# Rotary tables multiplied by the reciprocal roots on GpSimd, in a projection stage of one stage less

## What is computed

```python
def apply_rotary(x, cos, sin):
    x1, x2 = (x[..., :d], x[..., d:])
    return jnp.concatenate([x1 * c + x2 * s, -x1 * s + x2 * c], axis=-1)
...
q = (x @ Wq.T).reshape(B, T, 2 * H, hd)
k = (x @ Wk.T).reshape(B, T, 2 * H, hd)
v = (x @ Wv.T).reshape(B, T, H, 2 * hd)
q = apply_rotary(rmsnorm(q), cos, sin)
k = apply_rotary(rmsnorm(k), cos, sin)
```

## Time and profile before

| | |
|---|---|
| median of three runs | 691.15 us (689.38 to 691.51) |
| span of the profiled execution | 687.9 us (the page gives no other time of it) |
| busy in the span: TensorE, VectorE, ScalarE, GpSimd | 590.2, 530.8, 496.5, 326.7 us |
| granted TensorE clock, mean | 0.950 |
| projection stage, last instruction | near 115.5 us |

### The profile page before, as it was taken

One profiled execution on the slowest core, in us unless ns is written; L12 is line 12 of the kernel. 1 busy time (PEld: TensorE's weight loads), 2 busy tenths in 40 slices (PEclk: granted clock), 3 DMA queues, 4 the chain that ended last, 5 costly groups with the idle time before them and its releaser, 6 DMA issues. The chain is left out here.

```text
span 687.9 us, 15892 instructions
## 1 busy us (share of the span) xinstructions
PE 590.2 (86%) x4825; PEld 355.3 (52%) x4826; DVE 530.8 (77%) x1425; ACT 496.5 (72%) x843; POOL 326.7 (47%) x466
## 2 busy tenths in 40 slices
PE   3576765899999999999999999977999799999960
PEld 2465554233333333333333333375877589999960
DVE  3999998687978889797888877779798856555575
ACT  2367795798989989898998999923455467777741
POOL 0224345344534344452434544252477777776661
PEclk9799998799999999999999999998899979999995
DMA  8000001000544566644466650041122233333475
GB/s 218 16 16 31 20 13 61 1 1 2 102 91 74 82 116 116 115 88 91 63 106 116 116 106 12 1 157 59 59 82 74 80 82 102 95 103 91 131 208 166
DMA packets 76265, 56.06 MB, mean 81 GB/s; under 512 B 6528, under 2 KB 70848, under 8 KB 75968
## 3 DMA queue, kind: packets, MB, share of 16 engines
q1 hardware_dynamic: 70688, 46.01, 30.8%
q0 software_dynamic: 4352, 8.99, 3.9%
q10 hardware_dynamic: 1184, 0.56, 0.3%
HBM read 15.36 MB, written 28.65 MB: 64 GB/s over the span
## 5 line engine op out<-in xcount | busy, mean ns | idle before, releaser
L787 ACT ACTIVATE attend_prob<-attend_ring 128x1024 f32<-128x1024 f32 (+1 forms) x320 | 280.0, 951 | 16.4 <-PE attend_ring L933 14.4
L731 POOL TENSOR_SCALAR_AFFINE_SELECT attend_prob<-attend_prob 128x256 f32<-128x256 f32 x256 | 118.0, 485 | 141.4 <-ACT attend_prob L787 140.8
L953 PE MATMUL attend_ps_o<-attend_prob,attend_v_slot 128*32 128x512 f32 (+3 forms) x1536 | 156.6, 496 | 0.0
L933 PE MATMUL attend_ring<-attend_qk_slot 32*128 32x512 f16 (+3 forms) x672 | 80.1, 329 | 8.1 <-ACT attend_prob L787 6.3
L1907 POOL DMA_INDIRECT expert_outputs<-routed_linear_gated,routed_expert_goal_now x72 | 70.3, 977 | 29.7 <-issue 23.9
L1033 POOL DMA_INDIRECT slots<-rows,slot_index x64 | 62.1, 971 | 37.3 <-issue 33.2
L933 PEld LDWEIGHTS attend_ring<-attend_qk_slot 32*128 32x128 f16 x672 | 22.4, 91 | 106.7 <-ACT attend_prob L787 37.6
L1935 DVE TENSOR_TENSOR outed_linear_head_normed<-outed_linear_head_normed,routed_linear_ps_c 128x256 f32<-128x256 f32 x72 | 30.2, 420 | 41.3 <-ACT outed_linear_head_normed L2029 36.8
L953 PEld LDWEIGHTS attend_ps_o<-attend_prob,attend_v_slot 128*32 128x32 f32 x1536 | 33.7, 108 | 44.9 <-issue 37.7
L2076 PE MATMUL routed_linear_ps_c<-outed_linear_head_normed,head_turned 128*128 128x128 f32 x384 | 52.5, 281 | 1.1 <-ACT head_turned L2010 1.1
L369 POOL TENSOR_TENSOR project_parts_q<-project_rotated_q,project_parts_q 128x1024 f16<-128x1024 f32 x8 | 17.6, 2201 | 68.9 <-ACT project_parts_q L417 68.9
(11 more groups left out here) (291 smaller groups left out, 1281.8 us busy)
## 6 DMA issues: line engine op xcount, KB each, us to landing
slots<-attend_zeros SPq DMA_DIRECT2D x24, 715.0 KB, 10.2
attend_qk_slot<-qk_parts SPq DMA_DIRECT2D x14, 512.0 KB, 3.1
x_pairs<-slots SPq DMA_DIRECT2D x72, 65.0 KB
v_all<-expert_outputs SPq DMA_DIRECT2D x8, 512.0 KB, 5.5
xn_all<-project_xn SPq DMA_DIRECT2D x8, 256.0 KB, 2.3
w<-w_laid SPq DMA_DIRECT2D x1, 2048.0 KB, 7.8
rows<-rows SPq DMA_DIRECT2D x4, 512.0 KB, 3.8
out<-xn_all SPq DMA_DIRECT2D x8, 256.0 KB, 3.5
```

Of the source, the lines that this page charges most:

```text
L731: ins = nc.gpsimd.affine_select(out=edge, in_=edge, compare_op=ALU.is_ge, fill=0.0, base=0, pattern=[[0, 2], [1, P]], channel_multiplier=-1)
L787: nc.scalar.activation(probs(k, pair)[:, :, 0:width], scores[:, :, 0:width], ACT.Exp, scale=HD ** -0.5).then_inc(exp_made[u][pair], 1)
L933: ins = nc.tensor.matmul(dst[:, s * QC + at:s * QC + at + cols], qk[rows, T + j * P:T + (j + 1) * P], qk[rows, qc * QC + off:(qc + 1) * QC ...
L953: ins = nc.tensor.matmul(ps_o[RB * s:RB * (s + 1), off:QC], v4[slot][:, j, s], probs(k, s // 2)[:, s % 2, at:at + cols], start=j == 0, sto ...
```

## The change

`body` loses its fourth group: turns have a (u+2), b (u+1) and c (u), and run from -2 to 7. In a turn, a is normalised, b is projected and rotated, and c is split in two parts, transposed and copied.

- The reciprocal roots no longer multiply q and k. GpSimd multiplies the tables of cosines and sines by them (four products of 128x256, two for each half), behind c's low parts in its queue, and VectorE multiplies q and k from PSUM by the results (`turn_half`, four passes of 128x512). PSUM of half h is free for the next projection when `half_turned[h]` is counted.
- The sum of squares, the root and the reciprocal are cut in halves of two tiles.
- VectorE's order in a turn: b's sums of squares, b's first reciprocal, a's statistics, b's second reciprocal, a's normalised x, b's four passes and b's four sums.
- ScalarE's: b's first square and v, c's high part of q, b's second square and first root, c's high part of k, b's second root and v, a's root, then the copies as before, of c now.
- TensorE's: behind b's projection six idle products, then the wait for c's low parts and c's quads 0 and 1, a's transposes, three idle products (there were three ahead of a's transposes and six behind them), c's quads 2 and 3.
- ScalarE takes a root of one number ahead of turn -2. The 4-bit rounding, steps 3 to 6, comes behind turn 6.

The core of the diff; the statistics and the normalised x of a are moved into functions (`statistics`, `normalise`) with nothing else changed, and `keep_v` is the copy of v.

```diff
-        sdev, rstd, pad = sb("sdev", GT), sb("rstd", GT), sb("pad", 1)
+        sdev, rstd, pad, warm = sb("sdev", GT), sb("rstd", GT), sb("pad", 1), sb("root_loaded", 1)
...
-        qkn = sb("qk_normed", GT * HQK * HD)
+        cos_n, sin_n = sb("cos_normed", GT * HQK * HD // 2), sb("sin_normed", GT * HQK * HD // 2)
...
-        squared = sem("squared")
-        qkv_made, v_kept, half_normed = ([sem(f"{n}{h}") for h in range(2)] for n in ("qkv_made", "v_kept", "half_normed"))
-        summed, rooted, rrms_made = (sem(n) for n in ("summed", "rooted", "rrms_made"))
-        turned = sem("turned")
+        squared = [sem(f"squared{h}") for h in range(2)]
+        qkv_made, v_kept, half_turned = ([sem(f"{n}{h}") for h in range(2)] for n in ("qkv_made", "v_kept", "half_turned"))
+        cos_made, sin_made = ([sem(f"{n}{h}") for h in range(2)] for n in ("cos_made", "sin_made"))
+        summed, rooted, rrms_made = ([sem(f"{n}{h}") for h in range(2)] for n in ("summed", "rooted", "rrms_made"))
...
-            return bcast(r[:, :, at:at + HD // 2], 2, 2 * HQK)
-
-        def halves(x):
-            return x.rearrange("p (t n d) -> p t n d", t=GT, d=HD // 2)
+            return bcast(r[:, :, at:at + HD // 2], 2, HQK)
+
+        half = lambda h: slice(h * GT // 2, (h + 1) * GT // 2)
+        by_head = lambda x: x.rearrange("p (t n) -> p t n", t=GT)
+        per_head = lambda x: x.rearrange("p (t n d) -> p t n d", t=GT, d=HD // 2)
+
+        def of_half(x, h):
+            n = x.shape[1] // 2
+            return x[:, h * n:(h + 1) * n]
...
-                body(*[(u + d, (odd + d) % 2) if inner or 0 <= u + d < GROUPS else None for d in (2, 1, 0, -1)])
+                body(*[(u + d, (odd + d) % 2) if inner or 0 <= u + d < GROUPS else None for d in (2, 1, 0)])
...
-            for u in range(GROUPS - 3, GROUPS + 1):
+            for u in range(GROUPS - 3, GROUPS):
...
-            def body(a, b, c, d):
...
-                    dve.wait_ge(half_normed[1], g + 1)
-                    nc.vector.tensor_tensor(halves(qcos), halves(qkn), rope(odd, 0), ALU.mult)
-                    nc.vector.tensor_tensor(halves(qsin), halves(qkn), rope(odd, HD // 2), ALU.mult).then_inc(turned, 1)
...
-                    dve.wait_ge(squared, 2 * g + 2)
-                    nc.vector.tensor_reduce(ssum, sq.rearrange("p (n d) -> p n d", d=HD), AX.X, ALU.add).then_inc(summed, 1)
+            def body(a, b, c):
                 if b:
                     g, odd = b
-                    dve.wait_ge(rooted, g + 1)
-                    nc.vector.reciprocal(rrms, sroot).then_inc(rrms_made, 1)
-                    dve.wait_ge(rrms_made, g + 1)
...
-                        dve.wait_ge(v_kept[h], g + 1)
-                        tiles = slice(h * GT // 2, (h + 1) * GT // 2)
-                        ins = nc.vector.tensor_tensor(qkn.rearrange("p (t h d) -> p t h d", t=GT, d=HD)[:, tiles], qk_psum[:, tiles],
-                                                      bcast(rrms.rearrange("p (t h) -> p t h", t=GT)[:, tiles], 3, HD), ALU.mult)
-                        ins.then_inc(half_normed[h], 1)
+                        dve.wait_ge(squared[h], g + 1)
+                        nc.vector.tensor_reduce(of_half(ssum, h), of_half(sq, h).rearrange("p (n d) -> p n d", d=HD), AX.X,
+                                                ALU.add).then_inc(summed[h], 1)
+                    unit_lengths(b, 0)
+                if a:
+                    statistics(a)
+                if b:
+                    unit_lengths(b, 1)
+                if a:
+                    normalise(a)
+                if b:
+                    g, odd = b
+                    for h in range(2):
+                        turn_half(b, h)
+                    add_halves(b)
+
+            def unit_lengths(group, h):
+
+                dve.wait_ge(rooted[h], group[0] + 1)
+                nc.vector.reciprocal(of_half(rrms, h), of_half(sroot, h)).then_inc(rrms_made[h], 1)
+
...
+            def normalise(group):
+
+                g, odd = group
+                dve.wait_ge(sdev_made, g + 1)
+                nc.vector.reciprocal(rstd, sdev).then_inc(rstd_made, 1)
+                dve.wait_ge(rstd_made, g + 1)
+                once(dve, xn_saved[odd], (g - odd) * 8)
+                once(dve, x_turned, g - 1)
+                for j in range(GT):
+                    ins = nc.vector.tensor_scalar(xn[odd][:, j * P:(j + 1) * P], m.x[:, ds(g * GN + j * P, P)],
+                                                  moments[:, 2 * j:2 * j + 1], rstd[:, j:j + 1], ALU.subtract, ALU.mult)
+                ins.then_inc(normed, 1)
+
+            def turn_half(group, h):
+
+                g, odd = group
+                by_pair = lambda x: of_half(x, h).rearrange("p (t n s d) -> p t n s d", t=GT // 2, s=2, d=HD // 2)
+                numbers = qk_psum[:, half(h)].rearrange("p t n (s d) -> p t n s d", s=2)
+                dve.wait_ge(v_kept[h], g + 1)
+                dve.wait_ge(cos_made[h], g + 1)
+                nc.vector.tensor_tensor(by_pair(qcos), numbers, bcast(per_head(cos_n)[:, half(h)], 3, 2), ALU.mult)
+                dve.wait_ge(sin_made[h], g + 1)
+                nc.vector.tensor_tensor(by_pair(qsin), numbers, bcast(per_head(sin_n)[:, half(h)], 3, 2),
+                                        ALU.mult).then_inc(half_turned[h], 1)
+
+            def add_halves(group):
+
+                g, odd = group
+                for h in range(2):
+                    dve.wait_ge(half_turned[h], g + 1)
+                once(dve, k_low, g)
+                cs = qcos.rearrange("p (t w h s d) -> p t w h s d", t=GT, w=2, s=2, d=HD // 2)
+                sn = qsin.rearrange("p (t w h s d) -> p t w h s d", t=GT, w=2, s=2, d=HD // 2)
+                for w in range(2):
+                    r = rot[w].rearrange("p (t h s d) -> p t h s d", t=GT, s=2, d=HD // 2)
+                    nc.vector.tensor_tensor(r[:, :, :, 0], cs[:, :, w, :, 0], sn[:, :, w, :, 1], ALU.add)
+                    nc.vector.tensor_tensor(r[:, :, :, 1], cs[:, :, w, :, 1], sn[:, :, w, :, 0],
+                                            ALU.subtract).then_inc(rotated[w], 1)
...
-                if u == GROUPS - 1:
+                if u == GROUPS - 2:
...
-                if u == GROUPS:
+                if u == GROUPS - 1:
...
-            def body(a, b, c, d):
+            def body(a, b, c):
...
+                if b:
+                    g, odd = b
+                    if isinstance(g, int) and g == 0:
+                        pool.wait_ge(rope_in, 16)
+                    for h in range(2):
+                        pool.wait_ge(rrms_made[h], g + 1)
+                        once(pool, half_turned[h], g)
+                        lengths = bcast(by_head(rrms)[:, half(h)], 3, HD // 2)
+                        nc.gpsimd.tensor_tensor(per_head(cos_n)[:, half(h)], rope(odd, 0)[:, half(h)], lengths,
+                                                ALU.mult).then_inc(cos_made[h], 1)
+                        nc.gpsimd.tensor_tensor(per_head(sin_n)[:, half(h)], rope(odd, HD // 2)[:, half(h)], lengths,
+                                                ALU.mult).then_inc(sin_made[h], 1)
...
+            def square(group, h):
+
+                g, odd = group
+                act.wait_ge(qkv_made[h], g + 1)
+                nc.scalar.activation(sq.rearrange("p (t c) -> p t c", t=GT)[:, half(h)], qkv4[:, half(h), 0:2 * C],
+                                     ACT.Square).then_inc(squared[h], 1)
+
...
+            def root(group, h):
+
+                act.wait_ge(summed[h], group[0] + 1)
+                nc.scalar.activation(of_half(sroot, h), of_half(ssum, h), ACT.Sqrt, bias=m.eps_rms[:, 0:1],
+                                     scale=1.0 / HD).then_inc(rooted[h], 1)
+
+            def body(a, b, c):
+                if b:
+                    square(b, 0)
+                    keep_v(b, 0)
+                if c:
+                    g, odd = c
+                    act.wait_ge(rotated[0], g + 1)
+                    nc.scalar.activation(part[odd][0][:, :, 0:2], bcast(rot_h[0], 2, 2), ACT.Copy).then_inc(q_high, 1)
+                if b:
+                    square(b, 1)
+                    root(b, 0)
+                if c:
+                    g, odd = c
+                    act.wait_ge(rotated[1], g + 1)
+                    nc.scalar.activation(part[odd][1][:, :, 0::2], bcast(rot_h[1], 2, 2), ACT.Copy).then_inc(k_high, 1)
+                if b:
+                    root(b, 1)
+                    keep_v(b, 1)
                 if a:
                     g, odd = a
                     act.wait_ge(mom_made, g + 1)
                     nc.scalar.activation(sdev, moments.rearrange("p (t k) -> p t k", k=2)[:, :, 1], ACT.Sqrt,
                                          bias=m.eps_ln[:, 0:1]).then_inc(sdev_made, 1)
...
+                if c and not b:
+                    keep(c, 0)
...
-                    keep(d, 2)
+                    keep(c, 2)
...
-                if d:
```

(53 more changed lines are left out.)

75 lines of the change are left out of this document (8 added, 67 removed).

## The result

The kernel after takes 711.09 us (median of 4 runs, 708.82 to 712.04), the one before 691.33 us (4 runs, 689.38 to 691.56) on the same chip: a ratio of 1.0295, 95% interval 1.0276 to 1.0313. It is slower, as forecast, but by 20 us instead of 10, outside the range. The span goes from 687.9 to 706.7 us. The next stage begins at 134.09 us (GpSimd's first memset there) against 116.63 before, 17.5 us later, and what follows takes 572.6 us against 571.3. So the loss lies in the projection stage. I call the start of that memset the stage's end from here on.

The account below looks back on a forecast made before the run. VectorE bounded the old turn of 10.85 us; the new chain, 11.0, plus 1.35 for low clock gave 12.35. 27.2 + 6 x 12.35 + 10.75 + 8.3 = 120.35 against 110.91; 691.15 + 9.8 = 701 us, range 696 to 705.

Parts of the forecast that it names:

- The chain in ScalarE's order: Per turn from first square (S) through high part, both low parts, transposes and copies to the next: 10.99 us.
- The idle stretch of 3.5 us: TensorE stands still from the end of its idle products, S + 2.6, to k's low part, S + 6.1.
- the copies' wait of 2.4: ScalarE idles about 2.4 us each turn in front of the copy of the first quad.
- the products of 0.6: GpSimd's four new 128x256 table products, behind the low parts, 0.6 us each, bounds 0.52 to 1.04.
- the passes of 0.65: VectorE's four new 128x512 passes from PSUM, 0.65 us each, 2.6 us together.
- The clock: TensorE's clock falls in nearly every turn, 0.7 us behind the restart, for 3.4 us; the turn grows by 1.35 us.
- low at every restart: Rival: TensorE's clock is already low when it restarts, turns of 13.1 us, 706 us in total; chance 0.12.
- 12.35: Forecast length of a turn in us: 11.0 at full TensorE clock plus 1.35 for the low clock.
- L271 beside GpSimd: Normalising of x beside GpSimd's low-part instruction: VectorE might lose 0.7 us, within its slack, so nothing changes.
- Start: Early Sqrt table takes a 1.28 us load out, all counting; first square of turn 0, S(0), at 27.2 us.
- Six turns: Turns 0 to 5 at 12.35 us each, bringing the first square of turn 6, S(6), to 101.3 us.
- Tail: After S(6): last sums at 10.75 us, fp4 steps 8.3 (bounds 5.3 to 8.93), rest as now, 0.2 more for low parts.

Follow-up runs that it names:

- g1: Changed kernel with 18 idle TensorE products instead of 6 and the four table products on VectorE instead of GpSimd; ratio 1.0028 to the kernel before.
- g3: Changed kernel with 18 idle products instead of 6, plus a GpSimd fill of 1024 columns between the two low parts; ratio 1.0259 to the kernel before.
- e1: Changed kernel with 18 idle TensorE products instead of 6 ahead of the wait for the low parts; 696.77 us, ratio 1.0100 to the kernel before.
- e3: Kernel before with only the early Sqrt table load, a root of one number ahead of turn -2; 687.97 us against 689.95, ratio 0.9978.
- e4: Changed kernel with the four products of tables and reciprocals on VectorE instead of GpSimd; 704.15 us, ratio 1.0211 to the kernel before.
- g4: Changed kernel with 18 idle products, a's statistics and normalised x early in VectorE's turn, a's root behind ScalarE's first square; ratio 1.0152 to the kernel before.
- h3: Same as g4, but with a's root on ScalarE behind the high part of q; ratio 1.0115 to the kernel before.
- h1: Kernel before, four groups and old order, with GpSimd's table products, four passes from PSUM and the early table; 753.17 us against 756.40, ratio 0.9951.

## Why the prediction was right or wrong

The direction and the mechanism held; the size did not. By its steps:

- **The chain in ScalarE's order: right.** 10.99 us added up, 11.2 measured at full clock without GpSimd's products (g1). The idle stretch of 3.5 us was 3.60, the copies' wait of 2.4 was 2.38, the products of 0.6 were 0.61, the passes of 0.65 start every 0.60.
- **The clock: the step that failed.** I took a fall 0.7 us behind the restart, 3.4 us long, from the row before 96.49, and priced it at 1.35 us a turn. In the trace after, the fall comes between 57 and 58 us, ahead of the restart at 58.82, and the low level lasts to beyond 64 us. This is the rival that I gave 0.12, "low at every restart", with its 13.1 us a turn; the turns were 12.96 to 13.63. The row that I drew on showed a fall behind an idle stretch; I read its position relative to the restart as fixed. Why the fall comes ahead of the restart here, and behind it in before and in g3, no run shows. The Trainium skill (TensorE: Matmul & The Clock Gate, What's actually happening) says that the throttled state is the default and activity releases it; e1 bears this out, where added useless work took some 13 us off.
- **The difference of 1.10 us between 12.35 and 13.45**, for the turn shown: restart at S + 6.20 instead of 6.1 (+0.10); quads 0 and 1 up to x's transposes 1.75 us instead of 1.25 (+0.50); transposes of x 0.91 instead of 1.1, idle products 1.28 instead of 1.2 (-0.11 together); quad 2 0.86 instead of 0.6 (+0.26); 0.33 us from there to the copy, where 0.2 was allowed (+0.13); and 0.22 behind the copies, 0.18 of it the wait for the projection.
- **L271 beside GpSimd: seen, but sized at 0.7 us; it was 1.4** (2.52 against 1.11), and the prediction had it beside the low part of k only, where GpSimd's products cover most of it. In after it is nearly hidden: the transposes of x follow the quads without a wait at 60.57, just behind its end. With the clock held GpSimd's products cost 0.5 us a turn (e1 against g1).
- **Start: right within 0.8 us.** S(0) = 26.40, forecast 27.2. The first deviation finds its table loaded. That all of its 1.28 us counts was too much by e3, where the later turns start 0.67 us earlier.
- **Six turns:** 106.84 - 26.40 = 80.44 us, forecast 74.1: +6.3.
- **Tail: short by 2.1 us, as the difference of two errors.** The end came at S(6) + 27.25; the forecast has 120.35 + 5.72 = S(6) + 24.8, and 0.4 for late copies. The last sums ended where I had them (S(6) + 10.70). The fp4 steps took 7.11 us (117.54 to 124.65), where 8.3 was forecast: 1.2 less. But TensorE's last quads can't start on their end, as I had it: GpSimd's last low parts took 2.82 and 3.19 us and ended at 126.7, 2.05 us behind the fp4 steps, and the quads, which lay ahead of the fp4 steps' end before (108.55), came only then, at the low clock. From the end of the fp4 steps to the stage's end passed 9.4 us instead of 6.1: 3.3 more.

The sum: -0.8 + 6.3 + 2.1 = 7.6 of the 7.7 us by which the stage's end missed (17.5 against 9.8).

## What to carry to other kernels

Before a pipeline stage is taken out, look for which in-order queue will then wait for the engine that the stage hid, and for how long TensorE stands idle meanwhile; price the low clock for all the work behind the idle stretch, not from one earlier fall. When a change bundles several edits, try the parts in the old order: here the early table and the passes from PSUM gain, the new schedule loses. And place what lengthens beside GpSimd on VectorE, here the normalised x, where GpSimd is idle.

## What the runs showed of the hardware

The four f32 instructions 128x128 of the normalised x (tensor_scalar, SBUF to SBUF) took 1.11 to 1.12 us with GpSimd idle, 1.57 in e4 when only the end of a low part lay beside them, 2.52 beside the end of a low part and three products (after), 2.96 in g4, 3.42 in g3, 4.05 beside two low parts (h3). Singly: 0.33 us alone, 0.65 each behind products of 0.61, and one of 2.16 beside a low part of 2.12. GpSimd's own instructions did not lengthen there: its products start 0.57 us apart in after and in h1 alike. The passes with an operand in PSUM took 0.68 to 0.69 with or without it. The Trainium skill (SBUF — State Buffer, SBUF: two separate sides) describes the pair of ports that the two engines share as an exclusive lock held for a whole instruction; VectorE's single durations agree with that, while the other side of it, GpSimd waiting for VectorE, shows in no row of these turns. Only in the last turn, beside the fp4 steps and what follows them, did GpSimd lose: 2.82 and 3.19 us for 2.12.
